# Quantised layers of a small transformer: the turns written out, input rounding on ScalarE, hidden quantisation a turn later, one scale on GpSimd

## What is computed

```python
def rmsnorm(x, g):
    var = jnp.mean(x * x, axis=-1, keepdims=True)
    return x * jax.lax.rsqrt(var + EPS) * g
def activation_quant(x):
    s = 127.0 / jnp.clip(jnp.max(jnp.abs(x), axis=-1, keepdims=True), 1e-05)
    return jnp.clip(jnp.round(x * s), -128.0, 127.0) / s
def bitlinear(x, w, g):            # w is quantised to -1, 0, 1 times its mean size
    xn = rmsnorm(x, g)
    return jnp.einsum('bsh,oh->bso', activation_quant(xn), weight_quant(w))
y = bitlinear(layernorm(x), w_gate, g_gate)     # 256 -> 2 x 1024
gate, v = jnp.split(y, 2, axis=-1)
x = x + bitlinear(silu(gate) * v, w_down, g_down)   # 1024 -> 256
```

## Time and profile before

| | us |
|---|---|
| median of 3 runs | 740.92 (738.47 to 742.08) |
| span of the profiled execution | 741.3 |
| PE busy | 610.1 (82%) |
| DVE busy | 466.3 (63%) |
| ACT busy | 321.4 (43%) |
| POOL busy | 141.1 (19%) |
| `bitlinear_stage`, first `xr` to last statistics | 183.98 to 310.44 |

### The profile page before, as it was taken

How to read it: one execution, slowest core, us unless ns; L and a number is a source line. 1 busy time by engine, 2 the same in 40 slices (tenths; PEclk the granted TensorE clock), 3 DMA queues, 4 the chain that set the end, 5 groups by cost and what they waited for, 6 DMA issues and landing times. The chain is left out here.

```text
span 741.3 us, 10967 instructions
## 1 busy us (share of the span) xinstructions
PE 610.1 (82%) x3504; PEld 456.3 (62%) x3524; DVE 466.3 (63%) x910; ACT 321.4 (43%) x512; POOL 141.1 (19%) x164
## 2 busy tenths in 40 slices
PE   2678988885465555487499999999999999999996
PEld 1446656644122222366388888888888888888884
DVE  2667878787989999477545555555545545554553
ACT  2666676654276676355323232323232223322322
POOL 2252222454734435350000000000000000000000
PEclk9989999999589999599799999999999999999999
DMA  9200000000100000177231222321213222231121
GB/s 272 110 1 1 1 0 1 1 1 10 49 0 0 0 0 0 55 244 198 56 96 59 70 65 63 106 80 59 70 66 118 58 71 61 66 113 70 57 71 42
DMA packets 36818, 45.66 MB, mean 62 GB/s; under 512 B 10113, under 2 KB 24081, under 8 KB 36657
## 3 DMA queue, kind: packets, MB, share of 16 engines
q1 hardware_dynamic: 33696, 41.06, 18.5%
q0 software_dynamic: 1008, 3.67, 1.5%
q10 hardware_dynamic: 2080, 0.52, 0.4%
HBM read 40.91 MB, written 4.33 MB: 61 GB/s over the span
## 5 line engine op out<-in xcount | busy, mean ns | idle before, releaser
L1550 ACT ACTIVATE act_hi<-x_tok 128x512 fp32r<-128x512 f32 x88 | 55.6, 631 | 197.3 <-DVE x_tok L1583 197.3
L1579 DVE TENSOR_TENSOR x_tok<-psU,x_tok 128x512 f32<-128x512 f32 x88 | 60.9, 692 | 110.6 <-PE psU L1490 110.6
L1585 DVE TENSOR_TENSOR act_lo<-x_tok,act_hi 128x512 fp32r<-128x512 f32 x88 | 61.0, 693 | 63.8 <-ACT act_hi L1550 63.8
L1544 ACT ACTIVATE x_tok<-psG 128x512 f32<-128x512 f32 x88 | 52.8, 600 | 49.2 <-PE psG L1490 49.2
L1488 PE MATMUL psG<-h3T_hi,wg_lo 128*128 (+1 forms) x176 | 69.9, 397 | 2.5 <-PEq L1189 2.5
L1501 PE MATMUL psY<-act_hi,wd_lo 128*128 128x512 f32 x176 | 68.9, 392 | 1.6 <-DVE act_lo L1585 1.6
L1489 PE MATMUL psG<-h3T_lo,wg_hi 128*128 (+1 forms) x176 | 69.1, 393 | 0.0
L1490 PE MATMUL psG<-h3T_hi,wg_hi 128*128 (+1 forms) x176 | 69.0, 392 | 0.0
L1488 PE MATMUL psU<-h3T_hi,wu_lo 128*128 (+1 forms) x176 | 69.0, 392 | 0.0
L1489 PE MATMUL psU<-h3T_lo,wu_hi 128*128 (+1 forms) x176 | 69.0, 392 | 0.0
L1490 PE MATMUL psU<-h3T_hi,wu_hi 128*128 (+1 forms) x176 | 69.0, 392 | 0.0
(11 more groups left out here) (227 smaller groups left out, 1230.4 us busy)
## 6 DMA issues: line engine op xcount, KB each, us to landing
cw_rows<-cw_spill SPq DMA_DIRECT2D x80, 128.0 KB, 2.9
cw_rows<-cw_spill SPq DMA_DIRECT2D x16, 224.0 KB, 2.9
cw_rows<-cw_spill SPq DMA_DIRECT2D x16, 192.0 KB, 2.7
w_stage<-in_L_ffn_w_gate_dram SPq DMA_DIRECT2D x11, 256.0 KB, 4.2
w_stage<-in_L_ffn_w_up_dram SPq DMA_DIRECT2D x11, 256.0 KB, 3.2
cw_rows<-cw_spill SPq DMA_DIRECT2D x16, 160.0 KB, 2.6
wg_nat<-in_L_attn_w_gate_dram SPq DMA_DIRECT2D x1, 2048.0 KB, 16.6
x_spill<-x_tok SPq DMA_DIRECT2D x1, 2048.0 KB, 8.4
```

The costliest lines, as they stand in the source:

```text
L1544: nc.scalar.activation(a[s % 2][:, :], psG[s % 2][:, :], ACT.Silu).then_inc(s_silu, 1)
L1550: nc.scalar.activation(a_hi[s % 2][:, :], a[s % 2][:, :], ACT.Copy).then_inc(s_hi, 1)
L1579: nc.vector.tensor_tensor(a[s % 2][:, :], psU[s % 2][:, :], a[s % 2][:, :], ALU.mult).then_inc(s_t, 1)
L1585: nc.vector.tensor_tensor(a_lo[s % 2][:, :], a[s % 2][:, :], a_hi[s % 2][:, :].bitcast(F32), ALU.subtract).then_inc(s_lo, 1)
```

## The change

- The loop is written out: all turns are straight text with numbers known in advance (`need` waits only for counts above zero), and the register instructions, the credits and the copy of `dq` (L881) are gone.
- `round_input` moves from DVE to ACT, as an Identity activation with scale and bias, four tiles ahead; `xr` and `q_in` get two buffers.
- `hr` gets a second buffer, and `quantise_hidden` is called for tile n - 2 instead of n - 1; with it the down matmuls and the residual come a turn later (n - 3).
- `hidden_scale` stands right behind `hidden` on DVE, and `dqh` is computed on POOL into four columns.
- The first part of the inputs has four tiles instead of two, the second four instead of six.

The core of the diff:

```diff
-INPUT_PARTS = ((0, 2), (2, NT // 2), (NT // 2, NT))
+def need(eng, sem, count):
+
+    if count > 0:
+        eng.wait_ge(sem, count)
+
+
+INPUT_PARTS = ((0, 4), (4, NT // 2), (NT // 2, NT))
...
-                for part, (first, end) in enumerate(((0, 2), (2, NT))):
+                for part, (first, end) in enumerate(((0, 4), (4, NT))):
...
-        xr = b.sb("xr", [P, D])
-        q = b.sb("q_in", [P, D], BF16)
+        xr = b.sb("xr", [P, 2, D])
+        q = b.sb("q_in", [P, 2, D], BF16)
...
-                def round_input(n, par):
-
-                    dve.wait_ge(s_q, seen(n))
-                    nc.vector.tensor_scalar(xr[:, :], at(k.xg, n)[:, 0, :], column(k.rscale, n), ROUND, ALU.mult,
-                                            ALU.add).then_inc(s_xr, 1)
...
+                def quantise_input(n):
+                    need(dve, s_xr, n + 1)
+                    need(dve, s_qT, n - 1)
+                    nc.vector.tensor_scalar(q[:, n % 2, :], xr[:, n % 2, :], -ROUND, 127.0, ALU.add, ALU.min
+                                            ).then_inc(s_q, 1)
...
-                def largest(n, par):
-
-                    small.begin(n)
-                    dve.wait_ge(s_hg, seen(n + 1))
-                    small.done(nc.vector.tensor_reduce(hsmall[:, 0:1], hg[:, par, :], AX.X, ALU.max,
...
+                def hidden_scale(n):
+
+                    par = n % 2
+                    top, clip, inv = (hsmall[:, par, c:c + 1] for c in range(3))
                     rs = rms[:, par, 1:2]
-                    small.wait_last()
-                    dve.wait_ge(s_pool, seen(2 * n + 2))
-                    small.done(nc.vector.tensor_scalar(hsmall[:, 1:2], hsmall[:, 0:1], rs, 1e-5, ALU.mult, ALU.max))
-                    small.wait_last()
-                    small.done(nc.vector.reciprocal(hsmall[:, 2:3], hsmall[:, 1:2]))
-                    nc.vector.tensor_scalar(dqh[:, par:par + 1], hsmall[:, 1:2], k.wmean[:, 1:2], 1.0 / 127.0, ALU.mult,
-                                            ALU.mult)
-                    small.wait_last()
-                    dve.wait_ge(s_hr, seen(n - 1))
-                    nc.vector.tensor_scalar(hscale[:, par:par + 1], hsmall[:, 2:3], rs, 127.0, ALU.mult, ALU.mult
+                    need(dve, s_hg, n + 1)
+                    need(dve, s_dqh, n - 1)
+                    nc.vector.tensor_reduce(top, hg[:, par, :], AX.X, ALU.max, apply_absolute_value=True
+                                            ).then_inc(s_top, 1)
+                    need(dve, s_top, n + 1)
+                    need(dve, s_rms, n + 1)
...
+                def quantise_hidden(n):
+                    need(dve, s_hr, n + 1)
+                    need(dve, s_hqT, n - 1)
+                    nc.vector.tensor_scalar(hq[:, n % 2, :], hr[:, n % 2, :], -ROUND, 127.0, ALU.add, ALU.min
+                                            ).then_inc(s_hq, 1)
...
-                def turn(n, par, ahead, one, two, three):
-                    if one:
-                        hidden(n, par)
-                    if two:
-                        largest(n - 1, 1 - par)
-                    elif one:
+                    need(dve, s_x2, n + 1)
+                    nc.vector.bn_stats(k.xstats[:, n, :], k.x[:, n, :]).then_inc(s_rows, 1)
+
+                for n in range(3):
+                    quantise_input(n)
+                input_scales(nc, k, dve, 1)
+                for n in range(NT + 3):
+                    if n < NT:
+                        hidden(n)
+                    if 1 <= n <= NT:
+                        hidden_scale(n - 1)
+                    if n == 0:
                         input_scales(nc, k, dve, 2)
-                    if ahead == 2:
-                        round_input(n + 2, par)
-                        quantise_input(n + 2, par)
-                    if two:
-                        hidden_scale(n - 1, 1 - par)
-                    if three:
-                        residual(n - 2, par)
-                        statistics(n - 2)
-                    if two:
-                        quantise_hidden(n - 1, 1 - par)
-
...
+                def hidden_dequant(n):
+                    need(pool, s_clip, n + 1)
+                    need(pool, s_x2, n - 3)
+                    nc.gpsimd.tensor_scalar(dqh[:, n % 4:n % 4 + 1], hsmall[:, n % 2, 1:2], k.wmean[:, 1:2],
+                                            1.0 / 127.0, ALU.mult, ALU.mult).then_inc(s_dqh, 1)
+
+                for n in range(NT + 1):
+                    if n < NT:
+                        gained(n)
+                        inv_rms(n)
+                    if n > 0:
+                        hidden_dequant(n - 1)
...
+                def round_input(n):
+
+                    need(act, k.scale_step, SCALES[n])
+                    need(act, s_q, n - 1)
+                    nc.scalar.activation(xr[:, n % 2, :], k.xg[:, n, :], ACT.Identity, scale=k.rscale[:, n:n + 1],
+                                         bias=rounder[:, :]).then_inc(s_xr, 1)
+
...
-                def turn(n, par, ahead, one, two, three):
-                    if ahead:
-                        silu(n + 1, 1 - par)
-                    if three:
-                        hq_out(n - 2, par)
-                    if one:
-                        squares(n, par)
-                    if ahead == 2:
-                        q_out(n + 2, par)
-                    if two:
-                        rounded(n - 1, 1 - par)
-
+                def hq_out(n):
+                    need(act, s_hqT, n + 1)
+                    need(act, s_down, n - 1)
+                    nc.scalar.activation(hqT[:, n % 2, :, :], psH[:, :, :], ACT.Copy).then_inc(s_hqTsb, 1)
+
+                for n in range(3):
+                    round_input(n)
                 for n in range(2):
-                    q_out(n, n)
-                silu(0, 0)
-                all_turns(act, turn)
+                    q_out(n)
+                silu(0)
+                round_input(3)
+                for n in range(NT + 3):
+                    if n + 1 < NT:
+                        silu(n + 1)
+                    if n >= 3:
+                        hq_out(n - 3)
+                    if n < NT:
+                        squares(n)
+                    if n + 2 < NT:
+                        q_out(n + 2)
+                    if 1 <= n <= NT:
+                        rounded(n - 1)
+                    if n + 4 < NT:
+                        round_input(n + 4)
 
             @block.tensor
...
-                def turn(n, par, ahead, one, two, three):
-                    if ahead:
-                        up(n + 1, 1 - par, 0)
-                    if three:
-                        h_transposed(n - 2, par)
-                    if ahead:
-                        up(n + 1, 1 - par, 1)
-                    if three:
-                        down(n - 2, par)
-                    if ahead == 2:
-                        q_transposed(n + 2, par)
-
-                for n in range(2):
-                    q_transposed(n, n)
-                for half in range(2):
-                    up(0, 0, half)
-                all_turns(pe, turn)
+                q_transposed(0)
+                q_transposed(1)
+                up(0, 0)
+                up(0, 1)
+                q_transposed(2)
+                up(1, 0)
+                for n in range(NT + 3):
+                    if n >= 3:
+                        h_transposed(n - 3)
+                    if n + 1 < NT:
+                        up(n + 1, 1)
+                    if n >= 3:
+                        down(n - 3)
+                    if n + 3 < NT:
+                        q_transposed(n + 3)
+                    if n + 2 < NT:
+                        up(n + 2, 0)
 
 
 
```

More of the change, by code:

```diff
@@ L835, in bitlinear_stage @@
         psD = b.ps("psD", [P, D])
-        (s_xr, s_q, s_qT, s_qTsb, s_dq, s_gate, s_v, s_silu, s_hid, s_ssq, s_hg, s_pool) = (b.sem("b_" + n) for n in (
-            "xr", "q", "qT", "qTsb", "dq", "gate", "v", "silu", "hid", "ssq", "hg", "pool"))
-        (s_small, s_hscale, s_hr, s_hq, s_hqT, s_hqTsb, s_down, s_x2, s_rows, s_round, s_centred, s_held) = (
-            b.sem("b_" + n) for n in (
-                "small", "hscale", "hr", "hq", "hqT", "hqTsb", "down", "x2", "rows", "round", "centred", "held"))
-        def column(t, n):
-            return t[:, n:n + 1] if isinstance(n, int) else t[:, bass.ds(n, 1)]
-        def all_turns(eng, turn):
-            turn(0, 0, 2, True, False, False)
-            turn(1, 1, 2, True, True, False)
-            with eng.Fori(0, NT // 2 - 2) as g:
-                turn(2 * g + 2, 0, 2, True, True, True)
-                turn(2 * g + 3, 1, 2, True, True, True)
-            turn(NT - 2, 0, 1, True, True, True)
-            turn(NT - 1, 1, 0, True, True, True)
-            turn(NT, 0, 0, False, True, True)
-            turn(NT + 1, 1, 0, False, False, True)
```

(49 more changed lines are left out.)

154 lines of the change are left out of this document (48 added, 106 removed).

## The result

| | before | after |
|---|---|---|
| median | 740.34 us (738.47 to 742.08, 4 runs) | 718.68 us (718.25 to 720.0, 4 runs) |
| ratio, 95% interval | | 0.971 (0.9695 to 0.9724) |
| span of the profiled execution | 741.3 | 717.5 |
| last statistics of the stage end at | 310.44 | 289.67 |

The changed kernel is 21.7 us faster. The profiled execution took 719.02 us in all, 1.5 more than its span. Of the 23.8 us between the two spans 20.8 lie ahead of the end of `bitlinear_stage`. The other 3.0 lie behind it, in stages that the change doesn't touch; two executions of the changed kernel also differ by 3.3 us outside the stage (spans of 717.5 and 714.2, both with 94.2 us from `hid`(0) to the stage's last statistics), 2.0 of them behind it. So the 3.0 can be chance for the most part; that none of it is the change's isn't shown.

The account below looks back on a forecast made before the run. DVE was taken to set the pace, with turns of 6.85 us falling to 5.4. `hid`(15) at 273.4 plus 16.8 gave 290.2 against 310.4, 20.2 us less: 740.9 - 20.2 = 720.7, forecast 721 us, range 716 to 729.

Parts of the forecast that it names:

- held clip: In the steady turn, DVE's one-element clip is held by POOL's `hg`: turns of 5.9 us, 727 us; chance 0.15.
- POOL's followers: DVE's `hq` waits for POOL's instructions after `hg`: up to 0.9 us per turn, 732 us; chance 0.10.
- ACT: The Identity costs 0.8 us and ACT still waits for PE: ACT's turn near 5.9 us, 727 us; chance 0.05.
- a cold PE: PE stays at 1.2 GHz, with twelve turns at 7.6 us: slower, 748 us; chance 0.05.
- no gain: Written-out text does nothing or costs fetch time, or an unseen wait: 741 us; chance 0.05.
- parts 1 and 2: DVE's new turn without `xr`: q is held behind `hg` to 3.94 us after `hid` starts; `hq` starts at 3.86.
- part 3: DVE's steady turn, with `hq`, residual and statistics added: 5.34 to 5.62 us, taken as 5.4.
- part 4: Other engines keep up with 5.4 us: ACT 5.05 a turn with the Identity at 0.4, PE 3.65, POOL 5.0.
- parts 5 and 6: Start and turns: `hid`(0) at 195.3, `hid`(1) 200.4, `hid`(3) 209.0, ten turns of 5.4, two of 5.2, `hid`(15) 273.4.
- part 7: Stage end: from `hid`(15) to the last statistics 16.8 us, against 15.9 before.

Follow-up runs that it names:

- Experiment 4: The changed kernel with `xr` moved back from ACT to DVE, right ahead of q, two buffers kept: 722.1 us.
- experiment 7: The changed kernel with POOL's gain product `hg` on 512 of 1024 columns, its result unused, so the hidden gain isn't computed: 712.1 us.
- 8: The changed kernel with residual and statistics ahead of q on DVE, and down matmuls ahead of the up-layer's second half on PE, in every turn: 717.2 us.
- b_written_out: The kernel before with only the loop of the quantised layers written out as straight text: 738.8 us.
- experiment 1: The kernel before with DVE's small numbers, clip to `hscale`, ahead of `xr` and q: 740.7 us.
- experiment 6: The changed kernel with the hidden quantisation back in its old turn, down matmuls and residual a turn earlier: 720.3 us.

## Why the prediction was right

The forecast was 721 (716 to 729); 718.7 was measured, and the rivals (held clip, POOL's followers, ACT, a cold PE, no gain) didn't occur; PE's granted clock was 1.00 from 210 to 270 us. By its own parts:

1. **The hold moves on to q** (parts 1 and 2). Right: q 0.85 (0.9 foretold), its end 0.16 behind `hg`. Experiment 4 turns it over to `xr`, 7 and 8 remove it. The only deviation is that `hg` starts 1.35 behind `hid`, not 1.43, since the loop's register work is gone (1.36 in b_written_out); hq then starts at 3.78 instead of 3.86.
2. **The clip isn't held** (part 2's rival). Right, 0.21 beside `hg`, in every kernel where it stands there. By Mode 2×_2P of VectorE: DVE Perf Modes (the Trainium skill), read literally as in the prediction, it would take both ports, from which the prediction took that it would be held; the trace disagrees for one element. A tensor_scalar of four elements is held in the same trace (192.98, 0.67), and one of eight that starts just behind the end of `hg` isn't (199.28, 0.17).
3. **The turn, 5.34 to 5.62, taken 5.4** (part 3). 5.23. From hq's start it is 0.60, 0.50 and 0.35 to the next `hid`, 1.45, where 1.48 was the lowest sum; with 3.78 that makes 5.23. The low ends were the right ones, for all three gaps: the text is straight. Over eleven turns (nine of 5.23 and the two without q) 0.17 less are 1.9 us, the largest error in the sum.
4. **ACT, 5.05 a turn** (part 4). The Identity costs 0.65, 0.5 net, not 0.4. ACT is nearly the bound: 19.16 of 20 us, and 4.84 a turn when nothing else holds (experiment 7). Right in its result, with 0.4 us to spare. PE 3.65 a turn at full clock: 13.23 / 20 x 5.23 = 3.46.
5. **POOL's followers** (second rival). They don't hold DVE; the hold runs the other way, `rms` 0.71 behind `hq`. It costs nothing, since `dqh` is wanted two turns later and the next `hg` starts 1.19 us after POOL is free.
6. **The start** (parts 5 and 6). `hid`(0) at 195.51 for 195.3, `hid`(1) at 200.60 for 200.4, `hid`(3) at 209.60 for 209.0. The wait for the table load and the first `xr` was 1.80 (0.5 was put). That `hid`(0) is only 0.2 off is luck in part: the stage ahead grew less than foretold (DVE's first row of `bitlinear_stage` comes at 185.10 for 183.97, 1.1 later and not 1.9), and the rest cancelled. A term was missing ahead of `hid`(3): the hold lasts as long as `hg`, and `hg`(2) itself waits for its buffer until ACT's first `hr` is done, so it starts 0.6 later than in a steady turn (1.94 behind `hid`) and q is held to 1.41 (207.67); `hid`(2) also waits 0.20 for PE. The turn behind `hid`(3) took 5.92 where 5.4 stood, for the same reason (q 1.15) and for a residual that waits 0.30 for `psD`.
7. **`hid`(15)** at 272.62 for 273.4: the 1.9 of the shorter turns, less 0.5 in the slow one and 0.6 already lost at `hid`(3). The two without q take 5.03 (5.2 foretold): hq stands in q's place there and is held to 1.25.
8. **The end** (part 7). 17.1 for 16.8.

The sum was 20.2 and the end of the stage came 20.8 earlier. That the two agree so well is luck in part: 1.9 too much in the steady turns stands against 1.4 too little elsewhere. The sum was set against the median of before as if nothing lay around a span; after, 1.5 us do. By that the profiled execution of before took some 2 us more than its median, which neither helped nor hurt a difference of two ends in the same stage.

What the prediction didn't say, and the experiments show, is what the gain is made of. Its first sentence on the matter, "A microsecond that leaves a DVE turn therefore leaves the kernel", failed in experiment 1: 0.8 us less of `xr` gave nothing. Its sum came right because it built the new turn instruction by instruction and didn't subtract from the old one. Read down the table of stages: 115.7 to 103.3 for `hscale` early and `hr` ahead of `qT`; to 97.6 for straight text, the split of the inputs, the second buffers, the later `hq` and `dqh` together (3.3 of these 5.7 in the first three turns); to 94.2 for `xr` on ACT. How the 5.7 divide among them isn't settled: `dqh` is none of it, the later `hq` is worth 0.7 in the changed kernel (experiment 6), and neither the split nor the buffers were tried alone.

## What to carry to other kernels

A busy instruction that ends just behind one of another engine is a wait, and moving it away hands the wait to the next instruction of the kind; so build the new turn row by row instead of subtracting durations. Fill the hold with something that isn't held (here a residual that reads PSUM), and only in the turns where what it needs is already there. Before moving work between engines, look in each queue for an instruction that is ready and stands behind one that isn't: two such exchanges gave 12.8 us here, the move of the rounding 3.4.

## What the runs showed of the hardware that wasn't expected

- The hold between DVE and POOL goes both ways, and whichever starts first has it. POOL's one-element `rms` takes 0.19 us beside DVE's unheld instructions and 0.71 when it starts 0.01 us behind `hq` (0.56 in a_half_gain). SBUF — State Buffer (the Trainium skill), section "Who interferes with whom", says that whoever issues first gets the shared pair of ports for the whole instruction and the other blocks; these rows agree.
- DVE's tensor_scalar of 4 or 6 elements per partition is held by POOL's products (0.67, where eight elements free of them take 0.17); one of 1 element isn't (0.21), in the steady turns of every kernel here where it meets `hg`.
- The granted clock of PE can fall for a few us in the middle of the stage, in one execution and not in another: 0.50 (the lower level, 1.2 GHz) from 262 to 266 in b_written_out, 0.56 on average from 212 to 215.4 in a_residual_first, 1.00 (2.4 GHz) from 210 to 270 in the changed kernel. Ahead of the fall PE had been busy 8.30 of 15 us (240 to 255) in the first and 3.89 of 7 us (205 to 212) in the second. In b_written_out it cost one turn 0.7 us.
